# A fused attention and feed-forward kernel: joined causal scores, 11 instead of 12 half-matmuls, free choice of engine, new lists

## The reference

```
a:  q = x Wq (16 heads of 64), k, v = x Wk, x Wv (8 groups; two heads share one)
    y = softmax(causal(q k / 8)) v Wout + b + x;   x = layernorm(y)
b:  twice (layers 0, 1), with h = x whose features 64..127 come from the token before:
    q, k, v = h Wqkv (8 heads of 64); q, k normalized to length 1, scaled, rotated (xpos)
    attention in windows of 64 tokens, over the window itself and the one before
    x = x + o Wo
    h = layernorm(shifted x) * g + c;  a, g = h W1 + b1 (341 each);  x = x + (a * gelu(g)) W2 + b2
out = layernorm(x1 + x)
```

## Time and profile before

| | us |
|---|---|
| median of 3 runs (lowest, highest) | 1151.34 (1151.09, 1151.92) |
| the profiled execution | 1151.44 |
| its span, from the first to the last instruction | 1149.6 |
| busy TensorE multiplications / loads | 1132.4 / 820.2 |
| busy VectorE / ScalarE / GpSimd | 1040.9 / 1001.2 / 958.5 |

### The profile page before, as it was taken

One profiled execution on the slowest core, in us unless ns is written; L12 is line 12 of the kernel. 1 busy time (PEld: TensorE's weight loads), 2 busy tenths in 40 slices (PEclk: granted clock), 3 DMA queues, 4 the chain that ended last, 5 costly groups with the idle time before them and its releaser, 6 DMA issues.

```text
span 1149.6 us, 45236 instructions
## 1 busy us (share of the span) xinstructions
PE 1132.4 (98%) x17504; PEld 820.2 (71%) x17504; DVE 1040.9 (91%) x4019; ACT 1001.2 (87%) x3168; POOL 958.5 (83%) x950
## 2 busy tenths in 40 slices
PE   9999999999999999999999999999999999999987
PEld 7677666777678676777676776777767777666765
DVE  7898899999999899999989899998998989999984
ACT  6888889888899889889898998989888898997795
POOL 2787888889888898888978889888978898988855
PEclk9999999999999999999999999999999999999999
DMA  6001010000110100111001101001001010011010
GB/s 233 11 12 33 16 32 22 21 16 9 31 27 5 45 14 3 41 25 39 14 3 36 38 23 32 17 4 42 9 23 26 4 28 23 14 35 29 11 33 27
DMA packets 31094, 31.85 MB, mean 28 GB/s; under 512 B 12576, under 2 KB 21408, under 8 KB 30752
## 3 DMA queue, kind: packets, MB, share of 16 engines
q1 hardware_dynamic: 30448, 28.17, 9.3%
q10 hardware_dynamic: 432, 0.79, 0.2%
HBM read 10.07 MB, written 2.10 MB: 11 GB/s over the span
## 4 chain that ended last, share of the span: by engine, by line
PE 83%; DVE 6%; POOL 5%; issue 2%; ACT 2%; DMA 0%; SPq 0%; POOLq 0%; DVEq 0%; ACTq 0%
PE psum L496 39%; PE psum L535 11%; PE psum L571 11%; PE psum L548 7%; PE psum L649 5%; PE psum L680 4%; PE psum L631 2%; PE psum L664 2%; DVE prob L898 1%; POOL x_hat L1164 1%; POOL rnorm L1135 1%; PE psum L594 1%; DVE b_prob L980 1%; ACT b_prob L803 1%; POOL b_prob L1152 1%
## 5 line engine op out<-in xcount | busy, mean ns | idle before, releaser
L747 ACT ACTIVATE prob<-prob,negmax 128x512 f32<-128x512 f32 (+3 forms) x512 | 282.7, 558 | 16.1 <-DVE negmax L898 15.3
L898 DVE CUSTOM_DVE_ANT_0 prob<-psum,causal 128x512 f32<-128x512 f32 (+3 forms) x512 | 224.0, 484 | 11.5 <-PE psum L535 9.6
L1102 POOL TENSOR_SCALAR prob<-prob,rowinv 128x384 f32<-128x384 f32 (+1 forms) x256 | 161.2, 649 | 50.1 <-DVE rowinv L904 48.7
L803 ACT ACTIVATE b_prob<-b_prob,b_negmax 128x128 f32<-128x128 f32 x512 | 199.0, 395 | 0.8 <-DVE b_negmax L980 0.7
L496 PE MATMUL psum<-wqkv,h_t 128*64 128x512 f32 x768 | 190.8, 599 | 0.1
L535 PE MATMUL psum<-k_t,q_t 64*128 64x384 f32 (+3 forms) x1024 | 163.5, 443 | 0.7 <-DVE prob_t L910 0.6
L1122 POOL TENSOR_TENSOR r<-r 128x512 f32<-128x512 f32 x120 | 153.4, 1284 | 7.0 <-DVE r L938 6.9
L571 PE MATMUL psum<-prob_t,v 128*64 128x256 f32 x1280 | 153.1, 380 | 0.0
L980 DVE CUSTOM_DVE_ANT_0 b_prob<-psum,band,rnorm 128x128 f32<-128x128 f32 x512 | 145.8, 344 | 5.4 <-PE psum L649 4.9
L1152 POOL TENSOR_TENSOR b_prob<-b_prob,b_rowinv 128x1024 f32<-128x1024 f32 x61 | 116.0, 1902 | 27.7 <-DVE b_rowinv L1000 27.6
L1105 POOL TENSOR_TENSOR prob<-prob,rowinv 128x512 f32<-128x512 f32 x96 | 98.1, 1047 | 36.4 <-DVE rowinv L904 36.3
(11 more groups left out here) (104 smaller groups left out, 2725.6 us busy)
## 6 DMA issues: line engine op xcount, KB each, us to landing
vb_mid<-vb SPq DMA_DIRECT2D x112, 128.0 KB, 2.4
x_t<-in_x_t SPq DMA_DIRECT2D x8, 256.0 KB, 3.9
x_n<-in_x SPq DMA_DIRECT2D x8, 256.0 KB, 3.1
x<-x SPq DMA_DIRECT2D x64, 31.8 KB
out<-x SPq DMA_DIRECT2D x15, 128.0 KB, 1.8
wqkv<-in_wqkv SPq DMA_DIRECT2D x1, 1536.0 KB, 11.3
w<-in_w SPq DMA_DIRECT2D x1, 768.0 KB, 13.1
x<-x SPq DMA_DIRECT2D x48, 0.2 KB
```

Of the source, the lines that this page charges most:

```text
L747: last = af(pr, pr, ACT.Exp, bias=negmax[:, k % 4, o:o + 1], scale=-1.0, accum_out=rowsum[:, k % 4, o:o + 1])
L803: last = af(pr, pr, ACT.Exp, bias=b_negmax[:, a, o:o + 1], scale=-1.0, accum_out=b_rowsum[:, a, o:o + 1])
L898: vec.tensor_tensor_reduce(prob[:, k % PROBS, h, p * K:(p + 1) * K], bank[:, p * K:(p + 1) * K], causal[:, S - K:S], -E ** -0.5, 3.0e38, A ...
L1102: last = gp.tensor_scalar(pr, pr, rowinv[:, k % 4, h:h + 1], 1.0, ALU.mult, ALU.mult)
```

## The change

1. *Joined scores* (tiles 0 and 1 of a sequence, `JOINT`). Pairs are taken by twos. The queries of the even pair lie with their token halves swapped; `q_late` holds the second token halves of both pairs side by side. Three multiplications give what four halves gave: all queries of the even pair with the early K - 64 keys, the late queries of both pairs with the 64 late keys, and all queries of the odd pair with the early keys. The masked block is left out. The maximum reads the pieces in place with a second mask (swapped), and the values take one pair at a time.
2. *Feed-forward.* Of the third chunk's 85 units of the linear part 64 are computed with 128-wide operands, the two column halves taking one half of the tokens each; the other 21 sit in unused weight columns 96 to 116 of the gate part. The gate of the third chunk is three instructions instead of one.
3. *Takers.* Each evacuation (a_q, a_v, a_turn by halves, a_value, b_v, b_turn_qk and b_turn_p by halves, b_value) goes to ScalarE or VectorE as a letter of `TAKERS` says; sums of rotated q, scalings of layer b, normalizations and ends to GpSimd or VectorE (scalings ScalarE too). `settled` waits for the taker's semaphore.
4. *Lists.* All strings of `SCORE`, the banks and the warm steps (34 multiplications before, 31 after) are new.

```diff
@@ project_q, TensorE: the even pairs' queries swapped
+                tokens = x_t[:, b % 2, i * P:(i + 1) * P]
+                turned_tokens = tokens.rearrange("p (q n) -> p q n", q=2)[:, ::-1, :]
                 for c in range(4):
-                    last = halves(bank[:, c * P:(c + 1) * P], wq[:, 4 * h + c, :], x_t[:, b % 2, i * P:(i + 1) * P])
+                    moving = turned_tokens if i in JOINT and c % 2 == 0 else tokens
+                    last = halves(bank[:, c * P:(c + 1) * P], wq[:, 4 * h + c, :], moving)
@@ scores, TensorE
+                queries = q_t[:, (NT * b + i) % 2, :, :]
+                for p in range(0, np_, 2 if i in JOINT else 1):
+                    keys = k_t[:, b % 2, (c + p) // 2, 0:K]
+                    if i not in JOINT:
+                        for h in range(2):
+                            last = mm(banks[h][:, p * K:(p + 1) * K], queries[half(h), c + p, :], keys[half(h)], start=True, stop=True)
+                        continue
+                    early = keys[:, 0:K - E]
                     for h in range(2):
-                        last = mm(banks[h][:, p * K:(p + 1) * K], q_t[half(h), (NT * b + i) % 2, c + p, :],
-                                  k_t[half(h), b % 2, (c + p) // 2, 0:K], start=True, stop=True)
+                        mm(banks[h][:, even_at(i, p):even_at(i, p) + K - E], queries[half(h), c + p, :], early[half(h)], start=True, stop=True)
+                    for h in range(2):
+                        mm(banks[h][:, even_at(i, p) + K - E:even_at(i, p) + K], q_late[half(h), i, (c + p) // 2, :], keys[half(h), K - E:K],
+                           start=True, stop=True)
+                    backward = early.rearrange("p (x n) -> p x n", n=E)[:, ::-1, :]
+                    for h in range(2):
+                        last = mm(banks[h][:, odd_at(i, p):odd_at(i, p) + K - E], queries[half(h), c + p + 1, :], backward[half(h)], start=True, stop=True)
@@ value, TensorE
-                for p in range(0, max(np_, 2), 2):
+                for p in range(0, max(np_, 2), 1 if i in JOINT else 2):
...
+                            if i in JOINT:
+                                place, turned_probs = slice(p * P, (p + 1) * P), two_pairs(k % PROB_TS, np_, i, h, p - p % 2, j)[:, p % 2, :, :]
+                                if p % 2 == 0:
+                                    turned_probs = turned_probs[:, ::-1, :]
@@ ffn, TensorE
-                for part in (1, 0):
-                    last = halves(bank[:, (1 - part) * z:(2 - part) * z], w1[:, l, part, ch * P:(ch + 1) * P], f_t[:, 0:z])
+                last = halves(bank[:, 0:z], w1[:, l, 1, ch * P:(ch + 1) * P], f_t[:, 0:z])
+                if ch < CH - 1:
+                    last = halves(bank[:, z:2 * z], w1[:, l, 0, ch * P:(ch + 1) * P], f_t[:, 0:z])
+                else:
+                    for w in range(2):
+                        last = mm(bank[half(w), z:z + z // 2], w1[:, l, 0, ch * P:ch * P + E], f_t[:, w * z // 2:(w + 1) * z // 2], start=True, stop=True)
@@ project_q, ScalarE (the same on VectorE)
+                last = copy(q_t[:, (NT * b + i) % 2, 4 * h:4 * h + 4, :].rearrange("p c n -> p (c n)"), bank)
+                if i in JOINT:
+                    last = copy(q_late[:, i, 2 * h:2 * h + 2, :].rearrange("p d (x n) -> p d x n", n=E), late_of(bank))
@@ gate, VectorE, third chunk
+                    for w in range(2):
+                        gated(u_t[0:E, ch, w * z // 2:(w + 1) * z // 2], bank[half(w), z:z + z // 2], b1[half(w), l, 0, ch:ch + 1])
+                    last = gated(u_t[E:k, ch, 0:z], bank[REST:REST + k - E, 0:z], b1[REST:REST + k - E, l, 1, ch:ch + 1])
@@ settled
+        def settled(engine, name, *args):
+
+            maker = taker(name, *args)
+            engine.wait_ge(ready[name][maker], UP_TO.get((maker, name, args), 0))
@@ SCORE, TensorE, one line of the string before and after (S scores, T transposes of part a)
-        "QQKQSQKSSVVKKQQVKVTSTSPPTSOQQPTTSSTShPkqPPvOTTTSSSKPhtTSTSqkPTsTTSSSKQPPQOvTSTTtSSpshaPokqTSTTSSpQQvaPPoTTTSSStQVPsO"
+        "QQKQSQSKKSVVVQQVKKTTSTSSPPPQQOTSTSTShPqkPPvOTTSTSShKPTStTSkqPsTSTSTSvKPPQQOtTTTSSpShsaqkPoTSTSTSpQQvPaPoTTStSTSsPVQO"
```

More of the change, by code:

```diff
@@ L29 @@
 B2ROW = 96
+REST = 96
 MASKED = -1e30
@@ L79, in group_before @@
     return GROUPS[place] if place >= 0 else (layer, -1)
[L82 to L89, removed]
+ENGINE_OF = {"a": "act", "d": "dve", "p": "pool"}
+BOTH = ("act", "dve")
+MAY_TAKE = {"a_q": BOTH, "a_v": BOTH, "a_turn": BOTH, "a_value": BOTH, "b_v": BOTH, "b_turn_qk": BOTH, "b_turn_p": BOTH, "b_value": BOTH,
+            "b_rotated_q": ("pool", "dve"), "b_scale": ("pool", "act", "dve"), "b_norm": ("pool", "dve"), "end": ("pool", "dve")}
@@ new lines, in shared_work @@
+def shared_work():
+    halves_of = [(*k, q) for k in SEQUENCE for q in range(2)]
+    return {"a_q": [(b, i, h) for b in range(B) for i in range(NT) for h in range(2)], "a_v": [(b, i) for b in range(B) for i in range(NT)],
+            "a_turn": [(*u, q) for u in UNITS for q in range(2)], "a_value": [u for u in UNITS if DUO[u] == u], "b_v": SEQUENCE,
+            "b_turn_qk": halves_of, "b_turn_p": halves_of, "b_value": SEQUENCE, "b_rotated_q": SEQUENCE, "b_scale": SEQUENCE,
+            "b_norm": GROUPS, "end": [(g,) for g in range(len(SIZE))]}
@@ L95 @@
             "b_turn_f", "n": "b_ffn", "w": "b_w2", "~": "warm"},
[L96 to L100, removed]
[3 rows of a table removed]
+    "act": {"Q": "a_q", "K": "a_k", "E": "a_exp", "T": "a_turn", "V": "a_value", "A": "a_v", "h": "b_h", "s": "b_square_q", "q":
+            "b_square_k", "v": "b_v", "t": "b_turn_qk", "e": "b_exp", "u": "b_turn_p", "r": "b_turn_f", "g": "b_gelu", "a":
+            "b_value", "c": "b_scale"},
+    "dve": {"T": "tables", "Q": "a_q", "V": "a_v", "M": "a_max", "I": "a_inverse", "A": "a_value", "U": "a_turn", "Y": "a_y",
[5 rows of a table added]
             "end_deviation", "A": "end"},
@@ L112 @@
[L112 to L115, removed]
@@ L576, in out_a @@
                 pe.wait_ge(wout_in, 16)
-                pe.wait_ge(z_ready, nth("act", "a_value", last_value(b, i)))
+                for c in range(0, CA, max(PAIRS_OF[i], 2)):
+                    settled(pe, "a_value", b, i, c)
                 bank, = claim("a_out", b, i)
@@ L912, in residual_a, with end @@
+            def end(g):
+                a, z = g % 2 * GROUP, SIZE[g]
+                b, t = tile(FIRST[g])
+                dve.wait_ge(rs_e_ready, nth("pool", "end_deviation", (g,)))
+                for k in range(z):
+                    last = vec.tensor_scalar(x1[:, b % 2, t + k, :], x1[:, b % 2, t + k, :], mv_e[:, a + k, 0:1], rs_e[:, a + k:a + k + 1],
+                                             ALU.subtract, ALU.mult)
+                last.then_inc(end_dve, 1)
             def residual_a(b, i):
@@ L1035, in stats, with gated @@
                 last.then_inc(var_b_ready, 1)
+            def gated(gelu, value, bias):
+                return vec.scalar_tensor_tensor(out=gelu, in0=value, scalar=bias, in1=gelu, op0=ALU.add, op1=ALU.mult)
             def gate(l, g, ch):
@@ L1079, in _ @@
                          "b_wo": residual_b, "b_stats": stats, "b_gate": gate, "b_w2": w2_add,
-                         "end_stats": end_stats, "b_rotated_q": rotated_of_q})
+                         "end_stats": end_stats, "b_rotated_q": rotated_of_q, "a_v": project_v, "a_value": value, "b_v": value_in,
+                         "b_value": value_b, "b_scale": scale_b, "b_norm": norm_b, "end": end})
         @block.gpsimd
```

397 lines of the change are left out of this document (244 added, 153 removed), and 8 rows, old and new, of the table LETTERS.

## The result

The changed kernel took 1159.87 us (median of 4 runs, 1158.34 to 1161.17) beside 1151.44 us before in the same session (1151.09 to 1151.92): ratio 1.0072, 95% interval 1.0055 to 1.0090. It is slower by 8.4 us. I had forecast 1150.9, no change; the time lies inside the stated range, on the side that had 0.26.

What follows compares the result with a forecast made beforehand. TensorE's instruction stream was taken to bound the kernel up to 1050 us, then a chain of waits through GpSimd. +2.7 us on the stream and -3.1 at the end gave -0.4: 1150.9 us, range for 8 in 10 1138 to 1161.

Steps and rivals of the forecast that it cites:

- the side that had 0.26: Whole kernel: the outcome slower by over 0.2%, given chance 0.26.
- +2.7 us on TensorE's stream: TensorE's instruction stream: -6.8 + 6.4 + 0.6 + 0.4 + 3.1 - 1.0 us.
- the zero for everything beside TensorE up to 1050 us: VectorE, ScalarE and GpSimd up to 1050 us: moved work priced at zero because TensorE's stream hides it.
- Joined scores (+6.4, +0.6, +0.4): TensorE, tiles 0 and 1: +6.4 us for tile 0 scores, +0.6 for tile 1 scores, +0.4 for values.
- the 54 ns off before narrow weights: Tile 0 scores step: 54 ns less where the next step loads narrow weights, giving 1.29 us a step.
- The first rival: Narrow scores run at the rate of their columns: scores -6.2 us instead of +7.0, time 1137.7; chance 0.12.
- Feed-forward (-6.8): Third chunk on TensorE: 864 ns becomes 650 in 30 groups, plus single groups, -6.8 us; the surest term.
- Lists (+2.1) and takers (0) up to 1050 us: New order: +3.1 us for scores behind 64-wide steps, -1.0 for fewer tiling changes; work moved between engines zero.
- The end (-3.1): Last 30 us: GpSimd relieved of ends and normalizations, longer last gate gives back 0.5; -3.1 us, bounds 0 and -10.
- The second rival: Last 100 us: free choice of evacuating engine and lighter GpSimd take 7 us more, time 1143.9; chance 0.18.
- ScalarE becomes the bound (1162): Evacuations from 60 to 1050 us: ScalarE 94% full; if unfillable above 93%, +11 us, time 1162; chance 0.17.

Runs made afterwards that it cites:

- the 96-column pieces: Changed kernel with the first and second piece of tile 0's joined scores 96 columns wide instead of 64, surplus overwritten: 1159.08 us, ratio 1.0070.
- the best that computes everything: Kernel before with the shorter third chunk and its three gate instructions in only 7 of 34 groups: 1151.71 us, ratio 1.0005.

## Why the prediction was wrong

**Which step failed.** The sum was +2.7 us on TensorE's stream and -3.1 at the end. In the trace the body grew by 5.0 and the tail by 2.7. The larger failure is the end, 5.8 us off, where I let VectorE's new work be free and counted only what GpSimd loses. The smaller one is the zero for everything beside TensorE up to 1050 us, 2.3 us off. By medians the lists with takers and end miss by 5.25 us and the feed-forward edit by 3.5.

**Joined scores (+6.4, +0.6, +0.4): right.** Measured +7.55 and +7.8 against 7.4. The tile-0 step took 1.34 us, the value that 112 ns a pair gives without the 54 ns off before narrow weights; I had 1.29. The 32 tile-1 steps came to 31.0 us after 31.2 before (31.5 in the old lists), where I had +0.6; the values of both tiles took 0.5 us more in the old lists, where I had +0.4. A tile-1 step takes 0.93 us, or 1.02 ahead of a change of tiling as here:

```profile
351.05 0.54 PE L611 MATMUL psum<-k_t,q_t 64*128 64x192 f32 x4
351.43 0.33 PE L613 MATMUL psum<-k_t,q_late 64*128 64x64 f32 x4
351.60 0.55 PE L617 MATMUL psum<-k_t,q_t 64*128 64x192 f32 x4
352.07 1.10 PE L734 MATMUL psum<-qk_t 64*64 64x128 f32 x32
```

The first rival (58 ns, 1137.7 us) is refuted by the step's duration and by the 96-column pieces. The Trainium skill's rule that a load costs its columns over 1.2 GHz ("TensorE: Matmul & The Clock Gate", section "LDWEIGHTS (loading the stationary operand)") gives 107 ns for 128 columns; the trace agrees within 5 ns for these multiplications. It does not for transposes: their loads have 128 columns too, and their pairs follow each other after 63 ns on the median of 112 steps of 16. Its statement that a matmul may start before its load is complete ("Advanced Engine Details and Errata", section "Miscellaneous Facts") brings a run of such pairs no nearer to 58 ns here.

**Feed-forward (-6.8): right on TensorE, lost behind it.** The chunks save what I said (-5.5 to -5.8 us of body steps). I had written that the third gate's +22.7 us on VectorE cost nothing up to 1050 us because TensorE's stream hides it. That step failed: the edit brought -3.3 in the new lists and +8.2 in the old. The step times say where: in the old lists the body lost what the chunks had saved and 4.5 us more, in the new ones it is 6.5 us shorter with the edit (0.9 of it a shorter wait for a DMA) and the tail 1.7 longer, where I had 0.5. So in the changed kernel the gates were nearly hidden in the body; the old lists show what that hung on. The 913 of 990 busy us on VectorE are no slack for one result that comes 0.74 us later. In the kernel before, W2 began 1.68 us after its last gate on average and 0.40 at least, in none of 28 body groups within 0.15; with the edit alone it is 1.01 on average and 13 times within 0.15. The changed kernel has 1.03 and 3 times: the new lists alone give 0.7 us more from the third chunk to W2 than the old ones (4.5 against 3.8). This fits the gain there, but no run changed that distance alone. One group of the kernel before, on VectorE and on TensorE (start, us, what):

```profile
803.56 1.44 DVE L1041 SCALAR_TENSOR_TENSOR u_t<-psum,b,u_t 128x256 f32<-128x256 f32 x3
804.93 0.68 DVE L889 COPY v<-psum 128x512 f32<-128x512 f32 x1
```

```profile
805.53 1.48 PE L496 MATMUL psum<-w,u_t 128*64 128x128 f32 x24
```

and the same group with the edit alone, on VectorE and on TensorE:

```profile
806.42 1.95 DVE L1157 SCALAR_TENSOR_TENSOR u_t<-psum,b,u_t 128x256 f32<-128x256 f32 x5
808.40 0.69 DVE L988 COPY v<-psum 128x512 f32<-128x512 f32 x1
```

```profile
807.11 1.04 PE L533 MATMUL psum<-wo,o_t 128*64 128x128 f32 x16
808.43 0.77 PE L533 MATMUL psum<-w,u_t 128*64 128x128 f32 x10 [0.27 <-DVE u_t L1157]
```

Before, W2 began 0.53 us after its last gate without a wait. Here the projection's turn of 0.87 us ends at 807.98; W2 starts 0.45 us later, when the fifth gate is done. The evacuation of v behind the gates starts 1.98 us after their first start, where it had 1.37.

**Lists (+2.1) and takers (0) up to 1050 us: the parts right, the zero wrong.** With lists and takers alone, scores of tiles 2 and 3 behind transposes cost +3.5 us (I had +3.1) and part a's transposes of these tiles -1.6 (I had -1.0 for changes of tiling). But the body grew by 4.6 in all: +2.5 are key projections, of which one waits 3 us for the DMA of x_t, +1.2 are a_v steps, and the changed kernel shows both (+1.4, +1.5). I had counted no DMA of SyncE's new list and no step that takes a bank from a later evacuation. Of the 3.5 us that TensorE idles in the middle of the changed kernel, 1.4 and 0.7 are two waits for a normalization that VectorE now does, both of the slow kind that "The end" tells of.

**The end (-3.1): the takers right, the sum wrong.** They were worth 3.6 within the new order, but the tail is 2.7 us longer in the changed kernel and 2.8 with the lists alone, so the rest of the new end costs more than they bring. I priced only what the old chain showed on GpSimd, and let VectorE's part be free. Normalizations and ends there take 692 and 712 ns on average, where I took 0.3 us from a neighbouring row of 0.296. These averages mix two kinds. Of the 39, 19 take 0.30 to 0.35 us, as I had. The other 20 take 0.43 to 1.93 us, and each of them ends 0.08 to 0.09 us after the end of an operation of GpSimd over 512 or 1024 elements per partition that had begun before it. One pair of normalizations, GpSimd's work beside it, and TensorE behind:

```profile
1090.36 1.78 DVE L1051 TENSOR_SCALAR x_hat<-x,mv_b,rs_b 128x128 f32<-128x128 f32 x2
1090.80 1.26 POOL L1279 TENSOR_TENSOR r<-r 128x512 f32<-128x512 f32 x1
1092.20 0.34 PE L777 MATMUL psum<-ident,x_hat 64*128 64x64 f32 x4 [1.30 <-DVE x_hat L1051]
```

The second normalization started at 1090.85 and ended at 1092.14, 0.08 us after GpSimd. With GpSimd idle, two took:

```profile
1133.37 0.60 DVE L1051 TENSOR_SCALAR x_hat<-x,mv_b,rs_b 128x128 f32<-128x128 f32 x2 [0.21 <-POOL rs_b L1314]
```

The 20 slow ones hold 14 us above 0.34 each. TensorE's four waits for VectorE's normalizations in the tail make 3.5 us, two of them (1.4 and 1.3) behind such a collision; before, its two waits for GpSimd's normalizations there made 1.1. I had not looked for what else runs when VectorE takes this work over. No run moved GpSimd's operations out of the way, so what the collisions cost is read from the trace, not tried. VectorE's busy time rose by 11.6 us in all, where I had -10, and most of the difference is these 14 us. The second rival (1143.9) fell: the tail became longer, not shorter.

**ScalarE becomes the bound (1162): the time was near, the mechanism not.** ScalarE is busy 917.78 of 990 us (I had 931), and TensorE 986.49. The waits that TensorE has more of than before are for VectorE and a DMA.

**What stays open.** That the longer gate and the shorter chunk cost 7.6 us more together than singly is measured. That the lost distance between VectorE's last gate and W2 is the cause fits the counts above, but moving W2 away did not give the time back, and I did not find which later step sets it. How much of the tail's growth is the new order, how much the collisions with GpSimd and how much the gates wasn't isolated either. No version was found that beats the kernel before: the best that computes everything took 1151.71, the same time.

## What to carry to other kernels

Where in-order engines are busy over 90% and their order is fixed, "hidden" must be read from the distance of each result to its first reader, not from busy shares: 0.7 us more in one evacuation, against a least distance of 0.40 to its reader, cost 4.0 us, and 11.7 with the reader 0.21 us sooner (8.2 net of what that brought). Before work moves to another engine, look at what runs beside it there: the average of 692 ns stood for 0.34 undisturbed and up to 1.93 beside GpSimd. For narrow fp32 multiplications count loads, not columns. A gain on the busiest engine holds only as far as its suppliers were early, so try each part alone in both orders of work: the feed-forward edit changed its sign.

## What the runs showed of the hardware

- Behind a 128-column load of an fp32 multiplication a pair takes 112 ns, whether 64 or (in part) 96 columns stream past it; 58 behind a 64-column load. Pairs of transposes with 128-column loads follow each other after 63 ns.
- VectorE's gate costs 491 ns on 21 partitions x 256 and 473 ns on 128 x 256; 345 ns on 64 x 128: the width counts and not the partitions, so splitting by partitions makes it dearer.
- A normalization with two per-partition scalars, 128 x 128 in SBUF, takes 0.33 to 0.35 us on VectorE with GpSimd idle. Where GpSimd had begun an operation over 512 or 1024 elements per partition before it, it ended only 0.08 to 0.09 us after that one, up to 1.93 us in all (20 of 39 cases). On GpSimd it takes 808 ns on average.
